# More of the attention's probability tiles transposed through memory, in a two-batch attention and LoRA block

## The chip, the core and the metric

One core of one Trainium2 chip runs the whole program in one launch. The metric is the device time of a run in microseconds (us). All data is float32.

## The reference

The input x is [2, 1024, 512]: two batches of 1024 tokens. The block is a pre-norm attention and a gated low-rank layer, both with a residual:

```
xn = layernorm(x)
q = rmsnorm(xn @ Wq.T), 32 heads of 128; k = rmsnorm(xn @ Wk.T), v = xn @ Wv.T, 8 heads of 128 (4 q heads share one)
scores = q @ k.T / sqrt(128) + slope[h] * (key - query), only keys <= query
x = x + (softmax(scores) @ v) @ Wo.T
f = layernorm(x); gates = 8 * softmax(f @ Wr.T + br)
x = x + 2 * sum_h gates[h] * (f @ A[h].T) @ B[h].T
```

## The kernel before

**Groups.** Each batch has 8 key/value heads, and each of them with its 4 query heads is one group of work: groups w = 0 to 7 are the first batch, 8 to 15 the second. In a group the 1024 queries are 8 row tiles s = 0 to 7 of 128. For row s and head h, `scores` (PE; every product is recorded at L1077, the line of the helper that issues it) fills PSUM with s + 1 blocks of 128 keys, `max` (DVE, L972) adds the bias and takes the row maximum, `exp` (ACT, L773) exponentiates and sums, `invert` (DVE, L979) takes the reciprocal for two heads at a time, and `normalise` (POOL, L852) multiplies. Every matrix product is three matmuls in a rounded float32 form (fp32r): each operand is split into a high part and a low rest, and high x high, high x low and low x high are summed.

**A probability tile.** The product with v needs the probabilities with keys on the partitions. So block j of row s, for the four heads together 128 x 512, has to be transposed. There are 36 such tiles in a group, and each goes one of two ways:

- on PE: `turn.p.s.j` (L1164) is four 128 x 128 transposes into a PSUM bank, `high.p` (ACT, L760) copies it rounded, `low.p` (DVE, L950) subtracts for the rest. It uses one of 2 slots of the pair of buffers pT_hi and pT_lo.
- through memory: `send_p.s.h` (SP's queue, L615) writes head h of all of the row's tiles of this kind to a buffer in device memory, one DMA for each head. `fetch_p.s.j` (SP's queue, L626) waits until all four heads of the row have landed and reads the tile back as 32 x 32 blocks put in transposed places, in 4 DMAs of 64 KB in runs of 128 bytes, to a raw buffer. `flip_p` (DVE, L958) transposes within the 32 x 32 blocks, `upper_p` (ACT, L768) and `lower_p` (POOL, L858) make the two parts. Here the first batch has 3 raw buffers and 2 slots, the second 5 and 4. A fetch waits for the `lower_p` that last read its raw buffer, an `upper_p` for the `values` item that last read its slot.

The table MEMORY_TILES says which tiles of a row go through memory: 16 of 36 in each group of the first batch, 20 of 36 in the second. `values.s.j` (PE) is three matmuls of 512 columns that add the tile's part to o_ps; in a row the tiles that PE transposed come first. Then `o_high` (ACT, L794) and `o_low` (DVE, L1000) split the result, and `y.s` (PE) is 12 matmuls of 512 columns against Wo, added up by `add_y` (L1006).

**Work of the next group.** A group also makes the next group's q (`q.8.c` and `q.9.c`: its first two rows, each in four items of 3 matmuls), and k and v (`turn.kv.0` to `3`, 24 matmuls of 256 columns each, then `turn.k.0`, `turn.k.1`). `v_high` and the next group's `values` wait for the last `values` of this one, since v has one buffer. The first batch transposes the weights on PE (10 items `turn.wo`, `turn.wkv`, `turn.wq`) and keeps them in memory; the second reads them back.

**The order.** Nothing is scheduled at run time: PROLOGUE, GROUP_A (groups 0 to 6), BOUNDARY (group 7), FIRST_B (8), GROUP_B (9 to 14) and LAST (15) are lists of items, and `follow` gives every engine those of its own kind in the list's order. Each engine runs its queue in order and waits where an item's inputs aren't there. BOUNDARY also has the second batch's layernorm and the first one's FFN, FIRST_B a rest of that FFN, and LAST the second one's. The FFN's tensors arT, bT and f_x are first used in BOUNDARY, where `load_a` and `load_wr` (SP's queue, L644 and L647) start.

**Head and tail.** This text calls the stretch of a group from its first matmul of `scores.0.0` to the end of `scores.7.3` its head, and from there to the next group's `scores.0.0` its tail.

Of the kernel before, what the change touches and what calls it, by code (L numbers as in the profile page):

```python
# [1261 lines left out]
```

## Time and profile before

| what | value |
|---|---|
| runs: median (lowest to highest of 3) | 2074.18 us (2071.1 to 2074.81) |
| the profiled execution: its own time | 2071.61 us |
| its span, first to last instruction | 2069.8 us |
| busy: PE, DVE, ACT, POOL | 97%, 66%, 56%, 56% |
| mean busy share of the 16 DMA engines, two queues | 37.8% (SP's) + 14.2% (ACT's) |
| the chain that ended last: PE | 79% |
| granted TensorE clock, mean | 0.997 |

PE's busy time counts matmuls whose ends are modelled: back to back, a matmul's duration overlaps the next one's, so work is better read from the spacing of starts. A wait of a few tenths can hide in it. In a timeline, consecutive instructions of one kind are merged (x4 is four), and idle time in front of them stands in brackets with what ended it.

### The profile page before, as it was taken

The numbers are of one execution on the slowest core, as the hardware profiler recorded it, in microseconds if no ns is written. First come the engines' busy times: TensorE is split into PE (matmuls) and PEld (weight loads), VectorE is DVE, ScalarE is ACT, GpSimd is POOL, SyncE is SP. The second block draws the span as 40 slices with busy tenths as digits, with TensorE's granted clock in tenths as the row PEclk, the third lists the DMA queues.
The fourth block names the chain that finished last, engine by engine and source line by source line (L and its number), as shares of the span: only waits on it lengthen the run. The fifth ranks groups of instructions, "written<-read, shape, count | busy, mean of one in ns | idle before, by whom it ended". The sixth has DMA issues, their size and how long they took to land.

```text
span 2069.8 us, 33617 instructions
## 1 busy us (share of the span) xinstructions
...
## 2 busy tenths in 40 slices
...
GB/s 163 120 135 110 166 122 131 106 125 171 107 144 138 97 158 115 146 151 153 122 131 140 136 99 175 99 151 142 108 138 99 176 102 142 154 77 167 70 124 93
DMA packets 822668, 269.13 MB, mean 130 GB/s; under 512 B 618584, under 2 KB 766040, under 8 KB 822496
## 3 DMA queue, kind: packets, MB, share of 16 engines
q1 hardware_dynamic: 770592, 164.75, 37.8%
q10 hardware_dynamic: 51904, 102.24, 14.2%
...
HBM read 145.25 MB, written 121.63 MB: 129 GB/s over the span
## 4 chain that ended last, share of the span: by engine, by line
PE 79%; DVE 6%; issue 4%; SPq 3%; DMA 3%; POOL 3%; ACT 2%; DVEq 0%; POOLq 0%; ACTq 0%
PE s_ps L1077 17%; PE q_ps L1077 15%; PE o_ps L1077 14%; PE y_ps L1077 14%; PE turn_ps L1164 10%; PE turn_ps L1077 7%; SPq L626 3%; DMA p_bounce<-probs_odd 1%; POOL probs_odd L852 1%; DVE more_raw L958 1%; DVE p_raw L958 1%; DVE qn L983 1%; DMA more_raw<-p_bounce 1%; POOL more_lo L858 1%; ACT qn L782 1%
## 5 line engine op out<-in xcount | busy, mean ns | idle before, releaser
L852 POOL TENSOR_TENSOR probs_odd<-probs_odd,p_inv 128x256 f32<-128x256 f32 (+3 forms) x256 | 316.6, 1255 | 212.4 <-DVE p_inv L979 212.4
L852 POOL TENSOR_TENSOR probs_even<-probs_even,p_inv 128x128 f32<-128x128 f32 (+3 forms) x256 | 261.6, 1043 | 222.0 <-DVE p_inv L979 221.7
L858 POOL TENSOR_TENSOR pT_lo<-p_raw,pT_hi 128x512 fp32r<-128x512 f32 x176 | 232.5, 1328 | 150.2 <-ACT pT_hi L768 150.0
L972 DVE CUSTOM_DVE_ANT_0 probs_odd<-s_ps,rel 128x256 f32<-128x256 f32 (+3 forms) x256 | 209.4, 820 | 107.4 <-issue 106.1
L1077 PE MATMUL s_ps<-kT_hi,qT_hi 128*128 128x512 f32 (+3 forms) x768 | 276.9, 361 | 2.9 <-DVE neg_max L972 2.8
L1077 PE MATMUL s_ps<-kT_hi,qT_lo 128*128 128x512 f32 (+3 forms) x768 | 262.3, 342 | 0.0
L1077 PE MATMUL s_ps<-kT_lo,qT_hi 128*128 128x512 f32 (+3 forms) x768 | 261.7, 341 | 0.0
L773 ACT ACTIVATE probs_odd<-probs_odd,neg_max 128x256 f32<-128x256 f32 (+3 forms) x256 | 212.4, 831 | 64.7 <-DVE neg_max L972 63.4
L773 ACT ACTIVATE probs_even<-probs_even,neg_max 128x128 f32<-128x128 f32 (+3 forms) x256 | 184.5, 722 | 108.7 <-DVE neg_max L972 106.9
L972 DVE CUSTOM_DVE_ANT_0 probs_even<-s_ps,rel 128x128 f32<-128x128 f32 (+3 forms) x256 | 174.8, 687 | 102.6 <-issue 101.7
L950 DVE TENSOR_TENSOR pT_lo<-turn_ps,pT_hi 128x512 fp32r<-128x512 f32 x288 | 195.2, 680 | 52.7 <-ACT pT_hi L760 52.5
L760 ACT ACTIVATE pT_hi<-turn_ps 128x512 fp32r<-128x512 f32 x288 | 169.7, 596 | 88.4 <-PE turn_ps L1164 88.3
L1077 PE MATMUL q_ps<-wqT_hi,xnT_hi 128*128 128x512 f32 x512 | 214.4, 419 | 0.1
L1077 PE MATMUL o_ps<-pT_hi,v_hi 128*128 128x512 f32 x496 | 205.9, 415 | 7.3 <-DVE oT_lo L1000 7.0
L1077 PE MATMUL y_ps<-woT_hi,oT_hi 128*128 128x512 f32 x512 | 204.5, 399 | 6.8 <-DVE oT_lo L1000 5.5
L1077 PE MATMUL q_ps<-wqT_hi,xnT_lo 128*128 128x512 f32 x512 | 201.0, 393 | 0.0
L1077 PE MATMUL y_ps<-woT_hi,oT_lo 128*128 128x512 f32 x512 | 200.8, 392 | 0.0
L1077 PE MATMUL y_ps<-woT_lo,oT_hi 128*128 128x512 f32 x512 | 200.8, 392 | 0.0
L1077 PE MATMUL q_ps<-wqT_lo,xnT_hi 128*128 128x512 f32 x512 | 200.5, 392 | 0.0
L782 ACT ACTIVATE qn<-q_ps 128x128 f32<-128x128 f32 x512 | 134.7, 279 | 107.2 <-PE q_ps L1077 105.7
L1077 PE MATMUL o_ps<-pT_hi,v_lo 128*128 128x512 f32 x496 | 194.6, 392 | 0.0
L1077 PE MATMUL o_ps<-pT_lo,v_hi 128*128 128x512 f32 x496 | 194.2, 391 | 0.0
...
## 6 DMA issues: line engine op xcount, KB each, us to landing
...
more_raw<-p_bounce SPq DMA_DIRECT2D x256, 64.0 KB, 2.2
...
```

The costliest lines, as they stand in the source:

```text
L626: sp.dma_start(raw_p(n)[b * BLOCK:(b + 1) * BLOCK, :].rearrange("p (n j) -> p n j", j=BLOCK), blocks[b]).then_inc(p_fetched[n], 16)
L760: nc.scalar.activation(target, bank, ACT.Copy).then_inc(sems["high"], 1)
L773: nc.scalar.activation(row, row, ACT.Exp, bias=neg_max[:, s % 2, h:h + 1], scale=-1.0, accum_out=p_sum[:, s % 2, h:h + 1]).then_inc(sems[" ...
L782: last = nc.scalar.activation(qn[:, h, :], q_ps[:, h * HD:(h + 1) * HD], ACT.Square, scale=float(slopes[gg % NG * G + h]), accum_out=q_sum ...
L852: nc.gpsimd.tensor_tensor(row, row, p_inv[:, s % 2, h:h + 1].to_broadcast((P, L)), ALU.mult).then_inc(sems["normalise"], 1)
L858: nc.gpsimd.tensor_tensor(p_low(r), raw_p(raw_tile[w, s, j]), p_high(r).bitcast(F32), ALU.subtract).then_inc(sems["lower_p"], 1)
L950: nc.vector.tensor_tensor(target, bank, upper.bitcast(F32), ALU.subtract).then_inc(sems["low"], 1)
L958: nc.vector.transpose(raw, raw).then_inc(sems["flip_p"], 1)
L972: nc.vector.tensor_tensor_reduce(out=probs[s % 2][:, h, 0:L], in0=s_ps[:, at_col:at_col + L], in1=rel[:, S - L:S], scale=-float(slopes[w % ...
L983: nc.vector.tensor_tensor(qn[:], q_ps[:].rearrange("p (h d) -> p h d", h=G), q_inv[:].unsqueeze(2).to_broadcast((P, G, HD)), ALU.mult).the ...
L1077: last = nc.tensor.matmul(target, a, m, start=start and i == 0 and k == 0, stop=stop and i == len(pairs) - 1 and k == 2)
L1164: last = nc.tensor.transpose(bank[0:width, i * rows:(i + 1) * rows], source, ident[0:rows, 0:rows])
```

## The change

Three things.

First, MEMORY_TILES has three stages in place of two: groups 0 to 6 now send 20 of 36 tiles through memory (16 before), group 7 keeps its 16, groups 8 to 15 send 24 (20 before). In groups 0 to 6, `turn.p` 4.2, 5.2, 6.3 and 7.2 go from PE to memory; in groups 8 to 15, 2.1, 3.1, 6.2 and 7.1.

Second, groups 0 to 6 get two more raw buffers and one more slot, in the room of f_x, bT and arT, which are not in use yet (5 raw buffers and 3 slots). `load_a` and `load_wr` therefore wait for the last readers of those places in group 6. Group 7 has 3 raw buffers and 2 slots as before, the second batch 5 and 4 as before.

Third, all six lists have a new order. Their other items are the same ones, each as often as before.

```diff
-MEMORY_TILES = ({2: (2,), 3: (2, 3), 4: (3, 4), 5: (3, 4, 5), 6: (4, 5, 6), 7: (3, 4, 5, 6, 7)},
-                {2: (2,), 3: (2, 3), 4: (2, 3, 4), 5: (2, 3, 4, 5), 6: (3, 4, 5, 6), 7: (2, 3, 4, 5, 6, 7)})
+MEMORY_TILES = ({2: (2,), 3: (2, 3), 4: (2, 3, 4), 5: (2, 3, 4, 5), 6: (3, 4, 5, 6), 7: (2, 3, 4, 5, 6, 7)},
+                {2: (2,), 3: (2, 3), 4: (3, 4), 5: (3, 4, 5), 6: (4, 5, 6), 7: (3, 4, 5, 6, 7)},
+                {2: (1, 2), 3: (1, 2, 3), 4: (2, 3, 4), 5: (2, 3, 4, 5), 6: (2, 3, 4, 5, 6), 7: (1, 2, 3, 4, 5, 6, 7)})
...
-    MEMORY_SLOTS, RAW_TILES = (2, 4), (3, 5)
+
+    MEMORY_SLOTS, RAW_TILES = 2, 3
+    MORE_SLOTS, MORE_RAW = (1, 0, 2), (2, 0, 2)
...
+    def stage(w):
+
+        return 0 if w < NG - 1 else 1 if w < NG else 2
...
+    def place(n, of, always, more):
+
+        n %= always + more[of]
+        return n if n < always else n + sum(more[:of])
...
+        with nc.sbuf_tensor("f_x", [P, 2, DM], F32) as f_x, nc.sbuf_tensor("bT", [P, DM], F32) as bT, \
+                nc.sbuf_tensor("arT", [P, C, P + NE], F32) as arT:
+            pass
+        pairs_0 = [(sb(f"pT_hi_a{i}", [P, G * P], F32R), sb(f"pT_lo_a{i}", [P, G * P], F32R)) for i in range(MORE_SLOTS[0])]
+        raw_0 = [sb(f"p_raw_a{i}", [P, G * P]) for i in range(MORE_RAW[0])]
...
+        def ffn_place_free(engine):
+            for name in last_early_slots:
+                after(engine, "values", *name)
+            for name in last_early_raws:
+                after(engine, "lower_p", *name)
...
             def load_a(w):
+                ffn_place_free(sp)
...
             def load_wr(w):
+                ffn_place_free(sp)
```

Of the lists, the end of GROUP_B, first before, then after:

```diff
-    "values.5.4 max.7.3 fetch_p.6.6 normalise.7.1 turn.p.6.0 turn.p.6.1 exp.7.3 y.4 send_p.7.0 send_p.7.1 high.p.6.0 "
-    "invert.7.1 flip_p.6.3 normalise.7.2 upper_p.6.3 values.5.5 add_y.4 normalise.7.3 turn.kv.3 send_p.7.2 low.p.6.0 "
-    "o_high.5 square_q.8 o_low.5 flip_p.6.4 high.p.6.1 lower_p.6.3 send_p.7.3 low.p.6.1 values.6.0 flip_p.6.5 "
-    "high.kv.3 inv_q.8 turn.p.6.2 low.kv.3 values.6.1 high.p.6.2 inv_k fetch_p.7.2 y.5 upper_p.6.4 low.p.6.2 "
-    "upper_p.6.5 norm_q.8 flip_p.6.6 lower_p.6.4 fetch_p.7.3 norm_k upper_p.6.6 values.6.2 lower_p.6.5 turn.p.7.0 "
-    "fetch_p.7.4 values.6.3 flip_p.7.2 lower_p.6.6 values.6.4 upper_p.7.2 q.9.0 high.p.7.0 fetch_p.7.5 lower_p.7.2 "
-    "values.6.5 flip_p.7.3 low.p.7.0 values.6.6 q.9.1 fetch_p.7.6 o_high.6 turn.p.7.1 upper_p.7.3 o_low.6 q.9.2 "
-    "high.p.7.1 lower_p.7.3 add_y.5 values.7.0 fetch_p.7.7 low.p.7.1 y.6 flip_p.7.4 flip_p.7.5 upper_p.7.4 "
-    "upper_p.7.5 lower_p.7.4 flip_p.7.6 values.7.1 lower_p.7.5 add_y.6 values.7.2 flip_p.7.7 turn.q.8 upper_p.7.6 "
-    "values.7.3 lower_p.7.6 values.7.4 upper_p.7.7 values.7.5 high.q.8 lower_p.7.7 values.7.6 low.q.8 turn.k.0 "
-    "values.7.7 high.k.0 turn.k.1 o_high.7 q.9.3 v_high o_low.7 high.k.1 y.7 v_low square_q.9 low.k.0 inv_q.9 low.k.1 "
-    "add_y.7 "
...
+    "send_p.7.0 exp.7.3 send_p.7.1 values.5.4 fetch_p.6.5 invert.7.1 flip_p.6.2 normalise.7.2 values.5.5 low.kv.2 "
+    "q.8.2 o_high.5 q.8.3 high.p.6.0 normalise.7.3 send_p.7.2 upper_p.6.2 low.p.6.0 turn.kv.3 high.p.6.1 flip_p.6.3 "
+    "add_y.4 upper_p.6.3 lower_p.6.2 send_p.7.3 o_low.5 fetch_p.6.6 flip_p.6.4 lower_p.6.3 values.6.0 low.p.6.1 "
+    "upper_p.6.4 turn.p.7.0 flip_p.6.5 square_q.8 lower_p.6.4 fetch_p.7.1 y.5 high.kv.3 inv_q.8 upper_p.6.5 "
+    "fetch_p.7.2 high.p.7.0 lower_p.6.5 norm_q.8 values.6.1 low.kv.3 values.6.2 inv_k fetch_p.7.3 low.p.7.0 "
+    "values.6.3 flip_p.6.6 turn.q.8 flip_p.7.1 upper_p.6.6 values.6.4 fetch_p.7.4 norm_k upper_p.7.1 lower_p.6.6 "
+    "q.9.0 high.q.8 values.6.5 lower_p.7.1 values.6.6 flip_p.7.2 fetch_p.7.5 turn.k.0 flip_p.7.3 upper_p.7.2 turn.k.1 "
+    "o_high.6 q.9.1 lower_p.7.2 high.k.0 o_low.6 fetch_p.7.6 q.9.2 upper_p.7.3 flip_p.7.4 values.7.0 lower_p.7.3 "
+    "upper_p.7.4 q.9.3 high.k.1 fetch_p.7.7 values.7.1 lower_p.7.4 flip_p.7.5 values.7.2 low.q.8 upper_p.7.5 "
+    "values.7.3 add_y.5 lower_p.7.5 values.7.4 flip_p.7.6 y.6 upper_p.7.6 lower_p.7.6 flip_p.7.7 low.k.0 upper_p.7.7 "
+    "low.k.1 lower_p.7.7 values.7.5 add_y.6 values.7.6 values.7.7 o_high.7 square_q.9 o_low.7 v_high y.7 inv_q.9 "
+    "v_low add_y.7 "
```

## Rows read from the trace of the kernel before

**Rows 1.** Windows: group 1, the turn of the batches, groups 8 and 15; columns as headed
```profile
core 0: us, PE busy (x) PEld busy (x) DVE busy (x) ACT busy (x) POOL busy (x), PEclk, DMA share, GB/s
...
166.60:291.80 125.20, 124.42 (x702) 107.30 (x701) 82.06 (x199) 74.09 (x210) 67.80 (x66) 1.00 0.51 131
...
917.20:1063.50 146.30, 142.23 (x812) 120.37 (x811) 123.53 (x319) 77.16 (x224) 78.62 (x94) 1.00 0.52 138
1063.50:1190.20 126.70, 124.13 (x676) 104.92 (x675) 83.97 (x216) 69.39 (x203) 75.50 (x75) 1.00 0.58 144
...
1924.20:2069.80 145.60, 125.48 (x633) 99.31 (x632) 107.83 (x291) 65.20 (x179) 74.91 (x81) 0.96 0.44 102
```

**Rows 2.** Windows: head of group 14; tails of groups 10, 11, 12, 14, 4 and 8
```profile
1801.90:1888.60 86.70, 85.83 (x478) 74.87 (x478) 55.12 (x156) 51.54 (x155) 49.97 (x52) 1.00 0.52 132
...
1398.88:1435.12 36.24, 34.09 (x169) 27.77 (x167) 21.41 (x32) 17.05 (x44) 23.53 (x20) 0.95 0.62 126
1521.88:1556.12 34.24, 32.81 (x168) 26.47 (x167) 21.29 (x32) 17.17 (x44) 23.52 (x20) 1.00 0.62 129
1642.88:1679.61 36.73, 32.98 (x168) 26.48 (x167) 21.29 (x32) 16.95 (x44) 23.50 (x20) 1.00 0.59 122
...
1888.64:1924.23 35.59, 32.69 (x168) 26.58 (x167) 21.29 (x32) 16.95 (x44) 23.54 (x20) 1.00 0.56 109
630.22:667.57 37.35, 36.81 (x220) 32.04 (x219) 23.20 (x35) 18.41 (x47) 19.61 (x17) 1.00 0.46 104
1157.32:1190.17 32.85, 31.50 (x150) 24.82 (x149) 21.74 (x32) 17.26 (x42) 22.68 (x19) 1.00 0.64 131
```

**Rows 3.** Groups of instructions: shapes xcount | busy, mean ns | idle before it, releaser
```profile
L858 POOL TENSOR_TENSOR pT_lo<-p_raw,pT_hi 128x512 fp32r<-128x512 f32 x176 | 232.5, 1328 | 150.2 <-ACT pT_hi L768 150.0
...
L950 DVE TENSOR_TENSOR pT_lo<-turn_ps,pT_hi 128x512 fp32r<-128x512 f32 x288 | 195.2, 680 | 52.7 <-ACT pT_hi L760 52.5
...
L760 ACT ACTIVATE pT_hi<-turn_ps 128x512 fp32r<-128x512 f32 x288 | 169.7, 596 | 88.4 <-PE turn_ps L1164 88.3
L958 DVE STREAM_TRANSPOSE p_raw<-p_raw 128x512 f32<-128x512 f32 x224 | 155.5, 699 | 39.6 <-DMA p_raw<-p_bounce 39.6
...
L768 ACT ACTIVATE pT_hi<-p_raw 128x512 fp32r<-128x512 f32 x176 | 110.6, 630 | 131.0 <-DVE p_raw L958 78.4 <-PE o_ps L1077 52.1
...
L1164 PE MATMUL turn_ps<-ident,probs_odd 128*128 128x128 f32 x608 | 90.4, 274 | 7.8 <-DVE probs_odd L888 7.8
```

**Rows 4.** Timeline of PE, group 9: start us, us, operation xcount
```profile
1302.12 0.60 PE L1164 MATMUL turn_ps<-ident,qn 128*128 128x128 f32 x4
1302.48 0.48 PE L1077 MATMUL o_ps<-more_hi,v_hi 128*128 128x512 f32 x1
1302.79 0.40 PE L1077 MATMUL o_ps<-more_lo,v_hi 128*128 128x512 f32 x1
1303.03 0.39 PE L1077 MATMUL o_ps<-more_hi,v_lo 128*128 128x512 f32 x1
```

**Rows 5.** Timeline of SP's queue, group 14: sends and fetches of the last row
```profile
1893.13 3.35 SPq L615 DMA_DIRECT2D p_bounce<-probs_odd  x4
...
1900.54 2.75 SPq L626 DMA_DIRECT2D more_raw<-p_bounce  x4
...
1909.77 4.15 SPq L626 DMA_DIRECT2D more_raw<-p_bounce  x8
```

**Rows 6.** Timeline of SP's queue: the same fetches in groups 10, 11, 8 and 4
```profile
1412.15 1.91 SPq L626 DMA_DIRECT2D more_raw<-p_bounce  x4
...
1533.40 1.91 SPq L626 DMA_DIRECT2D more_raw<-p_bounce  x4
...
1164.54 4.64 SPq L626 DMA_DIRECT2D more_raw<-p_bounce  x8
...
639.53 14.84 SPq L626 DMA_DIRECT2D p_raw<-p_bounce  x20
```

**Rows 7.** Timeline of PE, group 14: the last values item
```profile
1919.00 0.50 PE L1077 MATMUL o_ps<-more_hi,v_hi 128*128 128x512 f32 x1 [1.23 <-POOL more_lo L858]
```

More of the change, by code:

```diff
@@ L335, in attention_lora_block @@
         plans.setdefault(w, group_a if w < NG else group_b)
+    def stage(w):
+        return 0 if w < NG - 1 else 1 if w < NG else 2
     def through_memory(w, s):
-        return list(MEMORY_TILES[w // NG].get(s, ()))
+        return list(MEMORY_TILES[stage(w)].get(s, ()))
     def values_order(w, s):
@@ L386, in attention_lora_block @@
     turned, sends = [], [0, 0]
-    flips, fetches, last_in_slot, in_raw = [0, 0], [0, 0], {}, {}
+    flips, fetches, last_in_slot, in_raw = [0] * 3, [0] * 3, {}, {}
+    def place(n, of, always, more):
+        n %= always + more[of]
+        return n if n < always else n + sum(more[:of])
     for w in range(-1, LAST_W + 1):
@@ L393, in attention_lora_block @@
             elif item[0] == "flip_p":
-                name, b = (w, *item[1:]), w // NG
-                p_slot[name] = TURN_SLOTS + flips[b] % MEMORY_SLOTS[b]
+                name, of = (w, *item[1:]), stage(w)
+                p_slot[name] = TURN_SLOTS + place(flips[of], of, MEMORY_SLOTS, MORE_SLOTS)
                 p_before[name] = last_in_slot.get(p_slot[name])
                 last_in_slot[p_slot[name]] = name
-                flips[b] += 1
+                flips[of] += 1
             elif item[0] == "send_p" and item[2] == G - 1:
@@ L402, in attention_lora_block @@
             elif item[0] == "fetch_p":
-                name, b = (w, *item[1:]), w // NG
-                raw_tile[name] = fetches[b] % RAW_TILES[b]
+                name, of = (w, *item[1:]), stage(w)
+                raw_tile[name] = place(fetches[of], of, RAW_TILES, MORE_RAW)
                 users = in_raw.setdefault(raw_tile[name], [])
@@ L408, in attention_lora_block @@
                 raw_uses[name] = len(users)
-                fetches[b] += 1
+                fetches[of] += 1
     def follow(work):
@@ L498, in attention_lora_block @@
             pass
-        more_hi = sb("more_hi", [P, 2, G * P], F32R)
-        more_lo = sb("more_lo", [P, 2, G * P], F32R)
-        more_raw = sb("more_raw", [P, 2, G * P])
+        pairs_2 = [(sb(f"pT_hi_b{i}", [P, G * P], F32R), sb(f"pT_lo_b{i}", [P, G * P], F32R)) for i in range(MORE_SLOTS[2])]
+        raw_2 = [sb(f"p_raw_b{i}", [P, G * P]) for i in range(MORE_RAW[2])]
+        with nc.sbuf_tensor("f_x", [P, 2, DM], F32) as f_x, nc.sbuf_tensor("bT", [P, DM], F32) as bT, \
[3 more added lines that the diff above has]
+        raw_0 = [sb(f"p_raw_a{i}", [P, G * P]) for i in range(MORE_RAW[0])]
+        sb("arT_rest", [P, C * (P + NE) - W512])
+        turned_pairs = [(pT_hi[:, i, :], pT_lo[:, i, :]) for i in range(TURN_SLOTS + MEMORY_SLOTS)]
+        turned_pairs += [(hi[:], lo[:]) for hi, lo in pairs_0 + pairs_2]
+        raws = [p_raw[:, i, :] for i in range(RAW_TILES)] + [raw[:] for raw in raw_0 + raw_2]
         b_raw = f_x[:, 0, :].rearrange("p (h o r) -> p h o r", o=C, r=RK)
@@ L508, in p_high @@
         def p_high(slot):
-            more = slot - TURN_SLOTS - MEMORY_SLOTS[0]
-            return pT_hi[:, slot, :] if more < 0 else more_hi[:, more, :]
+            return turned_pairs[slot][0]
         def p_low(slot):
-            more = slot - TURN_SLOTS - MEMORY_SLOTS[0]
-            return pT_lo[:, slot, :] if more < 0 else more_lo[:, more, :]
+            return turned_pairs[slot][1]
         def raw_p(n):
-            return p_raw[:, n, :] if n < RAW_TILES[0] else more_raw[:, n - RAW_TILES[0], :]
+            return raws[n]
+        early = [name for name in p_slot if name[0] < NG - 1]
+        last_early_slots = [[name for name in early if p_slot[name] == TURN_SLOTS + MEMORY_SLOTS + i][-1] for i in range(MORE_SLOTS[0])]
+        last_early_raws = [[name for name in raw_tile if name[0] < NG - 1 and raw_tile[name] == RAW_TILES + i][-1] for i in range(MORE_RAW[0])]
+        def ffn_place_free(engine):
[3 more added lines that the diff above has]
+                after(engine, "lower_p", *name)
         def x_source(b, t):
@@ L550, in attention_lora_block @@
         p_sent = [sem("p_sent_even"), sem("p_sent_odd")]
-        p_fetched = [sem(f"p_fetched{i}") for i in range(RAW_TILES[1])]
+        p_fetched = [sem(f"p_fetched{i}") for i in range(RAW_TILES + sum(MORE_RAW))]
         ident_ready = sem("ident_ready")
```

10 lines of the change are left out of this document (3 added, 7 removed), and 502 rows, old and new, of tables (BOUNDARY, FIRST_B, GROUP_A, GROUP_B).

## The prediction, made before the changed kernel ran

> **What bounds the kernel now.** I read the windows first, by group. PE is busy for 124.4 of the 125.2 us of a first-batch group, for 124.1 of 126.7 in group 8, and for 125.5 of 145.6 in group 15, whose end is a serial chain of the FFN [rows 1]. So PE sets the pace, and an instruction taken off PE pays, as long as PE doesn't then wait for what replaces it. I then cut the groups in two. A second-batch head takes 86.7 us and PE is idle for 0.9 of it; a second-batch tail takes 34.2 to 36.7 us, mean 35.7 of four shown, with 1.4 to 3.7 idle; a first-batch tail takes 37.35 with 0.5 idle [rows 2]. The heads repeat, the tails scatter: what varies is there. The timelines say why. The last `values` item of group 14 starts at 1919.00 after a wait for `lower_p` [rows 7], 30.36 us after `scores.7.3` ended at 1888.64 [rows 2]. Behind it lies row 7's way through memory: four sends, then nothing from SP until they have landed, then 24 fetches one after the other [rows 5]. The first batch is bound by PE's work, the second by PE's work plus a late last row.
>
> **What four tiles less cost PE.** The timeline shows one turn between matmuls [rows 4]: four transposes at 1302.12, the next matmul at 1302.48, the one after it 0.31 later where 0.24 is usual. That is 0.36 + 0.07 = 0.43 to 0.44 us for a tile. 28 tiles in the first batch and 32 in the second make 60 x 0.44 = 26.4 us, 1.76 a group: the gain if nothing new waits. The mean duration of one transpose is 274 ns [rows 3], but durations overlap, so I don't take it. The Trainium skill (TensorE: Matmul & The Clock Gate, Part 4: PE-mode transpose) gives about 275 ns for a transpose in one kernel's context; as the price of each of the 240 transposes that would be a gain of 66 us. The duration agrees, but the spacing of the starts is what PE gets back.
>
> **What replaces them.** On ACT 630 ns for 596, on DVE 699 ns for 680 [rows 3]: nothing, neither is the pace. On POOL 1.33 us a tile, new [rows 3]: 5.3 us a group on top of 67.8 in 125.2 [rows 1], covered by its idle time; should a `lower_p` stand before a `normalise` that PE awaits, it costs up to 1.33 there. On SP's queue a fetch is four issues: eight take 4.15 us [rows 5], with the gap 2.1 us a tile, or 8.5 us a group, and row 7's and others' sends grow by a sixth or so. SP only matters where a row waits for it, which is row 7. `load_a` and `load_wr` now wait, with group 7's loads and first sends queued behind them, for the last `values` of group 6 at most; group 7's first tile through memory belongs to row 2, many us later, so I take nothing for these two waits.
>
> **Row 7's chain.** From `scores.7.3` to the first fetch (call it F) group 14 takes 1900.54 - 1888.64 = 11.9 us; group 10 13.3, group 11 11.5 [rows 2, 5, 6]. What follows `values.7.7` in a tail is 35.59 - 30.36 = 5.2 us. So F to `values.7.7` is 18.5, 17.7 and 17.5 us, 17.9 on average with six tiles; a seventh adds 2.1. Two groups start earlier: group 4 at 639.53 - 630.22 = 9.3 us, and group 8, whose second four of eight issues at 1164.54 begin about 1167, at 9.7 [rows 2, 6]. In the list of group 8 `fetch_p.6.6` stands behind `send_p.7.3`, so it goes out while the sends travel; in GROUP_B it stood ahead of `send_p.7.0`. The new GROUP_B has it behind `send_p.7.3`, and `fetch_p.6.5` behind `send_p.7.1`. But row 6 has five fetches now, as many before the last send as before. The new F lies between group 8's 9.7 and the old mean of 12.2; I take 10.8, nearer to the order that it has.
>
> **Groups 9 to 14.** I count PE's items from `scores.7.3` to `values.7.7` in both lists. Before: 16 `values` (0.69 each, three starts of 0.23), 3 `y` (2.74), one `turn.kv` (2.8), 3 `q` (0.69), 7 turns (0.44) make 27.2 us, and the trace's 30.36 is that plus the waits. After: 6 `q` and 4 turns make 28.0. Two `q` items and two turns changed sides, so the head gets shorter by 1.4 and by nothing else. The chain needs 10.8 + 17.9 + 2.1 = 30.8 us against 30.4 in group 14 (and 35.7 - 5.2 = 30.5 in the mean of the four). That is over the 28.0 of work, so PE still waits there: the chain sets it, not the work. A group changes by -1.4 + 0.4 = -1.0 us, six by -6. The bounds: F at 9.7 gives -2.1 a group, which its present waits allow; F at 12.2 gives +0.4, at 13.3 +1.5. In the new order `y.7` follows `values.7.7` with nothing between; before, a turn and a `q` lay there. From the one to the other it was 5.2 - 2.7 = 2.5 us, of which the matmuls, `o_high` and `o_low` take 0.7 + 0.6 + 0.7 in a row (the last two like the same operations in [rows 3]), so `y.7` waited for `o_low` then too, and the empty place costs nothing more.
>
> **Groups 0 to 6.** The tail now has 29.5 us of PE work to `values.7.7`, counted the same way. Its chain is F = 9.3 to 9.7, plus 17.9 with six tiles and five raw buffers, as the second batch has: 27.6 us. It is covered by work, and the whole 1.76 comes out. Against that `load_wo` (1 MB) moves down next to row 6's fetches and `keep_wkv` up into the tail. The old trace doesn't show this meeting; the nearest rows are the spread of F in the second batch, up to 13.3. F over 11.6 would begin to cost. I take off 0.16: -1.6 a group, -11.2 for seven. Bounds -12.4 and, with F at 13.3 (31.2 us, the old tail's own), about 0.
>
> **The rest.** Group 8: by count the head is 5 us shorter and the tail has 7 tiles at F = 9.7, so 29.7 for 27.6 us; as at most 1.8 of work and its 2.6 idle can go [rows 1], I take -2 (0 to -3). Group 15: head 2.3 shorter, of which 1.8 is work; its seventh tile gives 1 back: -1.3 (+1 to -2.3). Group 7 has the same work in a new order and is idle for 4.1 us [rows 1]: 0, between -2 and +2. The prologue's new order of loads: 0, within 1.
>
> **The sum.** -11.2 - 6 - 2 - 1.3 = -20.5 us against the profiled execution's own 2071.6 (span 2069.8), so 2051. The runs' median lies 2.6 above that execution; for the median I say 2074.2 - 20.5 = **2053.7 us**, a ratio of 0.990.
>
> **Rivals.**
> - *The full price.* F falls to 9.7 in every second-batch group and nothing meets `load_wo`: -12.4, six times -1.8 to -2.1, -3, -2.3: about -29, 2045 us. For it: F in groups 4 and 8, and that the heads repeat. Against it: a longer send (seven tiles) and five fetches in row 6. 0.20.
> - *Given back in the tails.* F stays at 12.2 in the second batch: +0.4 x 6, groups 8 and 15 even, and the first batch gets half (-6): about -4 to -2, 2071 us. For it: the old tails, where all that scatters depends on this queue. 0.16.
> - *SP's queue becomes the bound (slower).* The fetches and sends of row 6 push F past 13; at 14 a regular group pays 14 + 20 - 30.4 - 1.4 = +2.2 us, six make 13, groups 8 and 15 another 4, and the first batch gives 11 of that back: +6, 2080 us; with the first batch's tail held up too, 2085. It decides at F of about 13, where eight groups lose what seven gain; group 10 was there [rows 6]. 0.12. The Trainium skill (VectorE: DVE Perf Modes, Rules for kernel authors) says to transpose 128 x 128 on TensorE where the result may go to PSUM, which speaks against this change. No row here shows a tile slower as such, only its last steps late.
> - That the change doesn't do what it says is unlikely: by count each GROUP list loses four turns and gains four of each item through memory.
>
> My forecast has 0.52.
>
> **The numbers.** A measurement of this kernel can tell about 0.2%, 4 us, from no change. Faster by more than that takes the forecast, the full price and a little of the third case: 0.76. Within it most of the third: 0.13. Slower: 0.11. The range runs from the full price with a small bonus in group 7, 2043, to the third case, 2071; my case's own range is 2048 to 2062.
>
> **What would show it.** Right: periods of 123.5 us in groups 0 to 6 with F near 9.5 and no wait before `values.7.7`; heads of 85.3 us in groups 9 to 14, F of 10 to 11.5, `values.7.7` at 30 to 31.5 us after `scores.7.3` and still waiting for `lower_p`; PE's starts 240 fewer; POOL busy 80 us more. Wrong: F at 12 or more, waits in the heads (a `values.2.1` or `values.3.1` that comes before its tile), POOL's `normalise` behind a `lower_p`, or a first-batch tail that waits for a fetch.

## The result: 1.2% slower, and the profile after

The changed kernel takes 2097.7 us (median of 4 runs, 2095.9 to 2099.1) against 2072.6 us (4 runs, 2069.4 to 2074.8) on the same chip: a ratio of 1.0122, 95% interval 1.0104 to 1.014. The forecast was 2053.7 us in a range up to 2071. The profiled execution has a span of 2094.7 us and a time of 2096.5, 24.9 more than the one before.

First the page of the changed kernel: instructions, SP's queue (q1), and the chain that ended last by engine and by line.

```profile
PE 2003.9 (96%) x10828; PEld 1696.4 (81%) x10828; DVE 1365.4 (65%) x3431; ACT 1161.2 (55%) x3314; POOL 1237.7 (59%) x1220
...
q1 hardware_dynamic: 928032, 196.22, 44.8%
...
PE 53%; SPq 15%; DMA 9%; issue 7%; DVE 7%; POOL 5%; ACT 3%; DVEq 0%; POOLq 0%; ACTq 0%
SPq L656 14%; PE s_ps L1109 13%; PE q_ps L1109 11%; PE y_ps L1109 10%; PE o_ps L1109 8%; PE turn_ps L1196 7%; DMA p_bounce<-probs_odd 4%; PE turn_ps L1109 3%; DMA p_bounce<-probs_even 2%; POOL probs_odd L884 2%; POOL probs_even L884 1%; DMA p_raw<-p_bounce 1%; SPq L645 1%; DMA p_raw_a<-p_bounce 1%; POOL pT_lo L890 1%
```

PE has its 240 starts fewer (11068 before) and POOL its 60 more, as the diff says. What is new is in the chain: PE's share was 79% and is 53%; SP's queue and the DMAs had 3% each and have 15% and 9%. `SPq L656` is the issuing of fetches. A quarter of the chain now runs through SP's queue and the DMAs instead of through PE's work.

Then the windows, by group: groups 1 and 2, 7, 8, 9, 12 and 15 of the changed kernel. The columns are those of [rows 1].

```profile
164.40:289.20 124.80, 123.31 (x686) 105.75 (x684) 81.82 (x199) 73.78 (x210) 73.61 (x70) 1.00 0.60 148
289.20:417.60 128.40, 123.76 (x688) 105.86 (x686) 81.84 (x199) 73.81 (x210) 73.59 (x70) 1.00 0.59 144
918.10:1062.00 143.90, 141.57 (x812) 120.14 (x811) 120.58 (x319) 77.66 (x224) 79.20 (x94) 1.00 0.50 130
1062.00:1193.70 131.70, 125.54 (x660) 105.29 (x659) 83.23 (x216) 69.25 (x203) 80.00 (x78) 0.97 0.67 166
1193.70:1319.50 125.80, 119.30 (x629) 100.63 (x628) 75.90 (x188) 69.21 (x199) 78.24 (x74) 0.99 0.62 145
1571.40:1696.70 125.30, 120.07 (x629) 101.75 (x628) 75.79 (x188) 69.16 (x199) 78.19 (x74) 0.97 0.62 143
1947.30:2094.70 147.40, 126.80 (x617) 98.64 (x616) 107.33 (x291) 65.18 (x179) 80.27 (x84) 0.95 0.50 115
```

Summed from the first `scores` of each group to that of the next, in both profiled executions: the prologue gains 1.5 us and group 7 gains 2.4; groups 0 to 6 take 878.1 us against 875.6 (+2.5); group 8 131.7 against 126.7 (+5.0); groups 9 to 14 753.7 against 734.1 (+19.6, 3.3 each); group 15 147.4 against 145.6 (+1.8). Together +25. (Groups 0 to 6 with this same list took 869.1 to 878.1 us in the twelve profiles that have it here, 873.6 on average; with the old list 875.6 and 876.1. So the first batch usually gives 2 us back, and this execution is its worst.) PE is idle for 5 to 6.5 us in a second-batch group.

The head of group 12, its tail, and the tails of groups 14 and 2:

```profile
1571.36:1657.22 85.86, 84.75 (x472) 73.53 (x471) 54.55 (x155) 52.03 (x155) 52.54 (x53) 1.00 0.57 140
1657.22:1691.45 34.23, 31.53 (x143) 25.41 (x141) 19.32 (x31) 14.54 (x34) 24.44 (x20) 0.90 0.75 142
...
1908.97:1942.09 33.12, 29.30 (x144) 23.05 (x142) 19.35 (x31) 14.55 (x34) 24.43 (x20) 1.00 0.76 145
377.30:411.52 34.22, 30.28 (x173) 25.80 (x171) 18.37 (x30) 14.95 (x48) 22.27 (x18) 1.00 0.74 154
```

These tails run from the end of `scores.7.3` to the start of `values.7.7`. Group 14's is 33.12 us where it was 30.36, and only 0.8 us of that is more work by the prediction's count (28.0 against 27.2). The heads are near the forecast (85.4 to 86.0 us in groups 9 to 14; 85.3 was said). So in these groups the loss is in the tails.

SP's queue says why. Group 12 of the changed kernel, where `scores.7.3` ended at 1657.22:

```profile
1655.06 4.05 SPq L656 DMA_DIRECT2D p_raw_b<-p_bounce  x8
1659.21 2.02 SPq L656 DMA_DIRECT2D p_raw<-p_bounce  x4
1661.34 1.04 SPq L645 DMA_DIRECT2D p_bounce<-probs_odd  x2
1662.48 3.56 SPq L656 DMA_DIRECT2D p_raw<-p_bounce  x4
1666.08 1.13 SPq L645 DMA_DIRECT2D p_bounce<-probs_odd  x2
1667.30 4.00 SPq L656 DMA_DIRECT2D p_raw<-p_bounce  x4
1672.04 4.02 SPq L656 DMA_DIRECT2D p_raw_b<-p_bounce  x8
```

Four issues are one fetch. Between 1655.06 and 1661.23 stand three fetches of row 6; the first two sends of row 7, whose first tile was normalised 0.3 us after `scores.7.3`, leave only at 1661.34, 4.1 after it. Then one more fetch of row 6, the last two sends at 1666.08, one more fetch, and at 1672.04 the first of row 7. F, from `scores.7.3` to there, is 14.8 us. A fetch that stands behind sends also takes longer to issue: 3.56 and 4.00 us for four, against 2.02. Over the six groups F is 13.4 to 14.8, 14.2 on average, where the kernel before had 11.5 to 13.3, 12.3 on average; in group 8 it is 16.7.

What ends F is told by the landings. The trace has the last send landed 0.01 to 0.02 us before the first fetch of row 7 in each of the six groups, and SP was through with issuing only 0.1 to 0.8 us before that: two things end almost together. The issue of the last send ends 10.1 us after `scores.7.3` on average (8.4 in the kernel before), and it lands 4.0 us later (3.8 before). The raw buffers are not what holds it. The first tile of row 7 takes the raw buffer of 6.2 now, but the `lower_p` that it waits for had ended 8.0 us after `scores.7.3` in all six groups.

The clock makes it a little worse. `y.7` of group 13, behind its wait for `o_low` (PE's timeline, and the window to the end of the group):

```profile
1819.13 0.50 PE L1109 MATMUL y_ps<-woT_hi,oT_hi 128*128 128x512 f32 x1 [1.41 <-DVE oT_lo L1032]
...
1820.32 0.63 PE L1109 MATMUL y_ps<-woT_lo,oT_hi 128*128 128x512 f32 x1
1820.74 0.63 PE L1109 MATMUL y_ps<-woT_hi,oT_lo 128*128 128x512 f32 x1
1821.17 0.63 PE L1109 MATMUL y_ps<-woT_hi,oT_hi 128*128 128x512 f32 x1
```
```profile
1819.10:1823.60 4.50, 4.47 (x13) 3.53 (x14) 1.23 (x1) 1.23 (x4) 1.21 (x2) 0.62 0.61 229
```

The starts are 0.43 us apart where 0.23 is usual: the granted clock fell to 1.2 GHz after a tail in which PE had waited, and these twelve matmuls cost 1.6 us more than in the groups without it. It happened in groups 11 and 13. Over the whole span the mean granted clock is 0.988, against 0.997. Where the fall lies inside a tail that waits anyway, as in group 12 (0.90), it costs little and fills the idle time: that tail shows only 2.7 us idle, group 14's at full clock 3.8.

### The profile page after: what moved, and what is told of

Read it like the earlier page. It is cut to its first block, busy times and chain, and to the rows that moved or that the text cites. A ratio compares the mean times of both kernels' runs of the same rounds, so it can differ in the third digit from the quotient of the medians.

```text
span 2094.7 us, 33555 instructions
## 1 busy us (share of the span) xinstructions
PE 2003.9 (96%) x10828; PEld 1696.4 (81%) x10828; DVE 1365.4 (65%) x3431; ACT 1161.2 (55%) x3314; POOL 1237.7 (59%) x1220
## 4 chain that ended last, share of the span: by engine, by line
PE 53%; SPq 15%; DMA 9%; issue 7%; DVE 7%; POOL 5%; ACT 3%; DVEq 0%; POOLq 0%; ACTq 0%
SPq L656 14%; PE s_ps L1109 13%; PE q_ps L1109 11%; PE y_ps L1109 10%; PE o_ps L1109 8%; PE turn_ps L1196 7%; DMA p_bounce<-probs_odd 4%; PE turn_ps L1109 3%; DMA p_bounce<-probs_even 2%; POOL probs_odd L884 2%; POOL probs_even L884 1%; DMA p_raw<-p_bounce 1%; SPq L645 1%; DMA p_raw_a<-p_bounce 1%; POOL pT_lo L890 1%
## 5 line engine op out<-in xcount | busy, mean ns | idle before, releaser
L1109 PE MATMUL s_ps<-kT_hi,qT_hi 128*128 128x512 f32 (+3 forms) x768 | 272.5, 355 | 3.2 <-DVE neg_max L1004 2.2
L890 POOL TENSOR_TENSOR pT_lo<-p_raw,pT_hi 128x512 fp32r<-128x512 f32 x129 | 167.8, 1306 | 110.8 <-ACT pT_hi L800 110.8
L1109 PE MATMUL y_ps<-woT_hi,oT_hi 128*128 128x512 f32 x512 | 205.8, 402 | 17.6 <-DVE oT_lo L1032 14.0
L1109 PE MATMUL q_ps<-wqT_hi,xnT_hi 128*128 128x512 f32 x512 | 218.6, 427 | 2.1 <-DVE qn L1015 2.1
L1109 PE MATMUL o_ps<-pT_hi,v_hi 128*128 128x512 f32 x434 | 183.2, 422 | 24.2 <-POOL pT_lo L890 15.0
L990 DVE STREAM_TRANSPOSE p_raw<-p_raw 128x512 f32<-128x512 f32 x216 | 150.7, 702 | 74.9 <-DMA p_raw<-p_bounce 74.0
L982 DVE TENSOR_TENSOR pT_lo<-turn_ps,pT_hi 128x512 fp32r<-128x512 f32 x228 | 155.5, 683 | 54.4 <-ACT pT_hi L792 53.9
L792 ACT ACTIVATE pT_hi<-turn_ps 128x512 fp32r<-128x512 f32 x228 | 134.6, 595 | 99.2 <-PE turn_ps L1196 98.9
L1109 PE MATMUL o_ps<-pT_hi,v_lo 128*128 128x512 f32 x434 | 172.3, 397 | 0.0
L1109 PE MATMUL o_ps<-pT_lo,v_hi 128*128 128x512 f32 x434 | 171.4, 395 | 0.0
```

The lines of the kernel that those rows point to most:

```text
L792: nc.scalar.activation(target, bank, ACT.Copy).then_inc(sems["high"], 1)
L890: nc.gpsimd.tensor_tensor(p_low(r), raw_p(raw_tile[w, s, j]), p_high(r).bitcast(F32), ALU.subtract).then_inc(sems["lower_p"], 1)
L982: nc.vector.tensor_tensor(target, bank, upper.bitcast(F32), ALU.subtract).then_inc(sems["low"], 1)
L990: nc.vector.transpose(raw, raw).then_inc(sems["flip_p"], 1)
L1109: last = nc.tensor.matmul(target, a, m, start=start and i == 0 and k == 0, stop=stop and i == len(pairs) - 1 and k == 2)
```

## The experiments

Ratios are to runs of the kernel before on the same chip. The change ran on another chip than the variants: the kernel before takes 2072.6 us there and 2069.7 to 2070.4 on theirs. Where a variant is compared with the change's 2097.7 us below, the gain is therefore 2 to 3.5 us smaller by the ratios. Three theories stood against each other: the queue theory (SP's queue issues the last row's sends and fetches late), the load theory (the core's DMA engines have too much to move in the tail, whichever queue it comes from), and the clock as a cause of its own.

### One batch alone, and two halves of the second batch

**e1_first_batch_only**: the lists and tables of groups 8 to 15 as before. **e2_second_batch_only**: the prologue and groups 0 to 7 as before. For e1:

```diff
-                {2: (1, 2), 3: (1, 2, 3), 4: (2, 3, 4), 5: (2, 3, 4, 5), 6: (2, 3, 4, 5, 6), 7: (1, 2, 3, 4, 5, 6, 7)})
+                {2: (2,), 3: (2, 3), 4: (2, 3, 4), 5: (2, 3, 4, 5), 6: (3, 4, 5, 6), 7: (2, 3, 4, 5, 6, 7)})
```

> Only the first batch has the change: PROLOGUE, GROUP_A, BOUNDARY and their table are the changed kernel's, FIRST_B, GROUP_B, LAST and the 20 tiles of groups 8 to 15 the old one's. Theory Q (the loss lies in the second batch's tails, where SP's queue issues the last row's sends and fetches too late): the parts of the first half, read from the two traces, are -1.5 us in the prologue, +2.4 in groups 0 to 6 and -2.4 in group 7, so 2071 us against 2072.6, a ratio of 0.998 to 1.001; the tails of groups 9 to 14 go back to 30.4 us from scores.7.3 to the last values item. Theory C (the loss is the lower TensorE clock, which comes with the smaller PE work anywhere): dips of the clock remain, half of the loss stays, about 2085 us.

> Only the second batch has the change (groups 8 to 15 with 24 tiles and their new lists; prologue, groups 0 to 7 as before). Theory Q: the whole loss, 5.0 us in group 8, 19.6 in groups 9 to 14 and 1.8 in group 15, so 2072.6 + 26 = 2099 us, a ratio of 1.012 to 1.014. Theory C, if the dips come from what the first batch does: half or less, 2085.

Measured: e1 2064.6 us, ratio 0.9973 (0.9958 to 0.9988); e2 2101.0 us, 1.0142 (1.012 to 1.0164). e1 is a little faster than its expectation (0.998 to 1.001), which took the first batch from the change's own execution, its worst. The clock theory's 2085 us is out for both: the first batch's part helps, the second's does all the harm. In e1 the first-batch groups come in two kinds: 123.65 us with F at 9.85 us, where no tail waits, and 125.3 to 127.2 with F at 11 to 13.9.

**e3_rows_2_3_back** and **e4_rows_6_7_back**: in groups 9 to 14 two of the four more tiles go back to PE, once the early ones (2.1 and 3.1), once the late ones (6.2 and 7.1). The tables of those groups:

```diff
 e3
-{2: (1, 2), 3: (1, 2, 3), 4: (2, 3, 4), 5: (2, 3, 4, 5), 6: (2, 3, 4, 5, 6), 7: (1, 2, 3, 4, 5, 6, 7)}
+{2: (2,), 3: (2, 3), 4: (2, 3, 4), 5: (2, 3, 4, 5), 6: (2, 3, 4, 5, 6), 7: (1, 2, 3, 4, 5, 6, 7)}
 e4
-{2: (1, 2), 3: (1, 2, 3), 4: (2, 3, 4), 5: (2, 3, 4, 5), 6: (2, 3, 4, 5, 6), 7: (1, 2, 3, 4, 5, 6, 7)}
+{2: (1, 2), 3: (1, 2, 3), 4: (2, 3, 4), 5: (2, 3, 4, 5), 6: (3, 4, 5, 6), 7: (2, 3, 4, 5, 6, 7)}
```

> The changed kernel, but in groups 9 to 14 tiles 2.1 and 3.1 are transposed on PE again; rows 6 and 7 keep their added tiles (22 through memory). Theory Q (only what SP issues around rows 6 and 7 counts): tails as in the changed kernel, 34.1 us from scores.7.3 to the last values item, and two turns more in each head, +0.9 us a group: 2097.7 + 5 = 2103 us. Theory L (the DMA engines' total load makes every transfer late): tails half-way back, 32.3 us, so 2092 us.

> The changed kernel, but in groups 9 to 14 tiles 6.2 and 7.1 are transposed on PE again; rows 2 and 3 keep their added tiles (22 through memory). Theory Q: first fetch of row 7 at 12 us after scores.7.3 and six tiles, so 30 to 31 us to the last values item, a group takes 121.5 to 122.5 us: 2097.7 - 6 x 3.6 = 2076 us. Theory L: half-way back, 2087 us. Were the lost time in the heads (rows 2 and 3 late), nothing would be won here: 2097 us or more.

Measured: e3 2104.3 us, 1.016 (1.0134 to 1.0186); e4 2067.9 us, 0.999 (0.9981 to 1.0). With two tiles fewer through memory in either, one mends nothing and the other gives back 30 us (27 by the ratios), 8 more than was expected. So it is not how much goes through memory in a group, but when. SP's queue in group 12 of e4 (`scores.7.3` ended at 1639.76):

```profile
1635.71 1.92 SPq L656 DMA_DIRECT2D p_raw<-p_bounce  x4
1637.72 2.02 SPq L656 DMA_DIRECT2D p_raw_b<-p_bounce  x4
1640.11 2.18 SPq L645 DMA_DIRECT2D p_bounce<-probs_odd  x2
1642.39 2.49 SPq L656 DMA_DIRECT2D p_raw_b<-p_bounce  x4
1644.93 1.97 SPq L645 DMA_DIRECT2D p_bounce<-probs_odd  x2
1647.00 7.71 SPq L656 DMA_DIRECT2D p_raw<-p_bounce  x12
```

The queue is through with two fetches of row 6 at 1639.74, before `send_p.7.0` is due, and each send leaves as its tile is normalised (0.35, 2.16, 5.17 and 6.76 us after `scores.7.3`). Row 7's first fetch is the second four of the last line, at 1650.2: F is 10.4. `values.7.7` then starts at 30.8 us without a wait of its own (PE is idle for 1.3 us of the tail, at two earlier `values` items), and groups 10 to 14 take 121.2 to 121.5 us at full clock; only group 9 takes 122.0. Over the six groups F is 9.9 to 11.0, 10.4 on average: the last send's issue ends 7.2 us after `scores.7.3`, and it lands 3.0 us later. e3's F is 13.6 to 14.8.

### The order of the queue

**e5_fetch_behind_sends** and **e6_sends_early** keep 24 tiles and change SP's order in groups 9 to 14 alone. SP's items from row 6's sends on:

```diff
 e5
 send_p.7.1
-fetch_p.6.5
 send_p.7.2
 send_p.7.3
+fetch_p.6.5
 fetch_p.6.6
 e6 (on top of e5)
 fetch_p.5.3
+send_p.6.0
 fetch_p.5.4
+send_p.6.1
 fetch_p.5.5
-send_p.6.0
-send_p.6.1
 send_p.6.2
 send_p.6.3
 fetch_p.6.2
 fetch_p.6.3
-fetch_p.6.4
 send_p.7.0
 send_p.7.1
+fetch_p.6.4
 send_p.7.2
```

> All of the change stays, 24 tiles too; only fetch_p.6.5 moves in the list of groups 9 to 14 from behind send_p.7.1 to behind send_p.7.3. Queue theory (what fetches stand ahead of row 7's last send sets F): send_p.7.3 goes out at 6.8 to 7.5 us after scores.7.3 instead of 9.5, F falls from 14.1 to about 11.5, values.7.7 comes at 31.5: 2.6 us a group less, 16 in all, about 2082, or 2077 if the half-speed stretches of the clock go with the waits. Load theory (the bytes and packets of 24 tiles keep the DMA engines busy, whatever the order): F stays within 0.5 of 14, 2095 to 2098.

> As the one before, with two more places changed: fetch_p.6.4 behind send_p.7.1, and send_p.6.0 and 6.1 ahead of fetch_p.5.4 and 5.5. Queue theory: all eight sends go out as their tiles are normalised, send_p.7.3 at 6.8; ahead of row 7 still stand two or three fetches of row 6 (2.1 us each), so F is 11 to 12.5 and the time 2076 to 2082; the sends were not the larger part, the fetches are. Load theory: 2095 to 2098.

Measured: e5 2095.4 us, 1.0122 (1.0103 to 1.0141); e6 2093.9 us, 1.0112 (1.0091 to 1.0133). Both expectations of the queue theory missed. Group 12 of e5 (`scores.7.3` ended at 1652.81):

```profile
1656.66 3.67 SPq L645 DMA_DIRECT2D p_bounce<-probs_odd  x4
1660.43 7.63 SPq L656 DMA_DIRECT2D p_raw<-p_bounce  x8
1668.16 4.15 SPq L656 DMA_DIRECT2D p_raw_b<-p_bounce  x8
```

The last send left at 1659.57, 6.76 us after `scores.7.3` and as early as it can; but the two fetches behind it took 7.63 us to issue where eight issues take 4.15 in the next line, and F is 15.4. The sends had landed 1.3 us before that, so here it is the queue alone that ends F. In e6 the two fetches took 6.01 us and F is 13.4:

```profile
1663.17 6.01 SPq L655 DMA_DIRECT2D p_raw<-p_bounce  x8
```

What stood before the sends now stands behind them, stretched. Over the six groups F is 14.7 on average in e5 and 13.1 in e6, of 14.2. So the order is worth at most 1.1 us of F, while taking one fetch out (e12, below) is worth 3.3. e6 won its 1.1 us in the tails and lost them elsewhere: its heads are 1.3 us longer (PE is idle for 1.6 to 3.0 us of each, 0.9 to 1.2 in the change), and `y.7` ran at half clock in four groups instead of two.

### The same bytes on two queues

Both are e4 with 256 KB more in each of groups 9 to 14, in runs of 128 bytes, from a weight in memory to a scratch in memory that nobody reads: on SP's queue as four DMAs, or on ACT's as one.

```diff
 e7, in send_p
+                if (s, h) == (NT - 1, 2) and NG < w < LAST_W:
+                    for b in range(NBLK):
+                        sp.dma_start(extra[b * BLOCK:(b + 1) * BLOCK, :].rearrange("p (n j) -> p n j", j=BLOCK),
+                                     Wq[0:W512, b * BLOCK:(b + 1) * BLOCK].rearrange("(n b) j -> b n j", b=BLOCK)).then_inc(extra_done, 16)
 e8, in exp
+                if (s, h) == (NT - 1, 3) and NG < w < LAST_W:
+                    act.dma_start(extra.rearrange("p (n j) -> p n j", j=BLOCK),
+                                  Wq[0:16 * P, 0:BLOCK].rearrange("(n b) j -> b n j", b=P)).then_inc(extra_done, 16)
```

> The variant with 22 tiles in groups 9 to 14 (2067.9 us) plus, ahead of send_p.7.2 in each of these six groups, four extra DMAs on SP's queue of 64 KB in runs of 128 bytes (DRAM to DRAM, data that nobody uses): the issue work and the bytes of one fetch. Queue theory: send_p.7.2 and 7.3 and all behind them are 2.1 us later, 12.6 us in all, 2080. Load theory: the same, since the bytes are the same.

> The same 256 KB in runs of 128 bytes at the same moment, but issued as one DMA by ACT ahead of exp.7.3 instead of four on SP. Queue theory: SP's queue holds nothing more, so F stays at 10 to 11 and the time at 2067 to 2071; only what ACT itself loses to issuing counts. Load theory: as the one before, about 2080, since the DMA engines have the same packets to move at the same moment.

Measured: e7 2080.3 us, 1.0043 (1.0026 to 1.006); e8 2069.0 us, 0.9993 (0.9983 to 1.0002). On SP's queue the four cost 12.4 us, on ACT's the one cost 1.1, which is inside the spread of e4's runs. Queue and number of DMAs changed together; four DMAs of 64 KB on ACT's queue were not tried here. Group 12 of e7 (`scores.7.3` ended at 1647.93):

```profile
1653.10 3.42 SPq L650 DMA_DIRECT2D extra<-in_L_attn_Wq  x4
1656.57 1.21 SPq L653 DMA_DIRECT2D p_bounce<-probs_odd  x2
1657.87 7.57 SPq L664 DMA_DIRECT2D p_raw<-p_bounce  x12
```

F is 12.8 to 14.1 in e7 and 10.2 to 11.5 in e8. The total of e7 is what was expected, but not by that sum: since 2 us of F were covered in e4, `values.7.7` is only 0.0 to 2.0 us later, 4.6 in all six groups. Another 5.5 came in `y.7` of groups 11, 13 and 14, which ran at half clock (1.6 us in each of the first two), and 2.6 in group 8, where nothing had been added.

### Two fetches on ACT's queue, and one tile at a time

**e9_two_fetches_on_act** keeps 24 tiles and issues `fetch_p.6.5` and `6.6` from ACT in groups 9 to 14.

```diff
 e9, in the functions of SP and of ACT
+    ON_ACT = ((6, 5), (6, 6))
             def fetch_p(w, s, j):
+                if (s, j) in ON_ACT and NG < w < LAST_W:
+                    return
+            def fetch_p(w, s, j):
+                if (s, j) in ON_ACT and NG < w < LAST_W:
+                    fetch_on(act, w, s, j)
```

> The change as it is, 24 tiles, but in groups 9 to 14 the eight DMAs of fetch_p.6.5 and 6.6 are issued by ACT, behind exp.7.3, instead of SP. If it is SP's own queue that is full (what its order could not mend), F falls by the two fetches, from 14.1 to 10 to 11, values.7.7 comes at 30.5 to 31.5 instead of 33.5, and the time is 2075 to 2082; ACT has 4.2 us of issuing more, which it has free time for. If what counts is the packets that the core's DMA engines must move in those microseconds, whichever queue they come from, F stays near 14 and the time at 2094 to 2098.

Measured: 2083.0 us, 1.0067 (1.005 to 1.0085), 14.8 less than the change as it is (11 by the ratios). That is 1 us outside what the queue theory gave for the time (2075 to 2082), and F, 12.8 to 14.0, is well outside what it gave for that (10 to 11). The load theory's time (2094 to 2098) is missed by 11. Group 12 (`scores.7.3` ended at 1651.48), SP's queue and ACT's:

```profile
1655.68 4.14 SPq L657 DMA_DIRECT2D p_bounce<-probs_odd  x4
1664.48 4.04 SPq L624 DMA_DIRECT2D p_raw_b<-p_bounce  x8
```
```profile
1653.01 1.41 ACTq L624 DMA_DIRECT2D p_raw<-p_bounce  x3
1654.45 2.83 ACTq L624 DMA_DIRECT2D p_raw<-p_bounce  x5
```

The sends are all issued by 1659.82 and then SP has nothing to issue for 4.7 us: it waits for the sends to land. F is 13.0, of 14.8; over the six groups 13.3, of 14.2. The last send is issued 1.9 us earlier than in the change (8.3 us after `scores.7.3`, not 10.1), but it takes 5.0 us to land instead of 4.0. So the issuing could be taken from SP's queue, and half of what that gave was lost in the landing. `values.7.7` comes 1.2 us earlier, 7 us in six groups. The rest of the gain can't be read from this profile, which is of the slowest of e9's four runs. The windows of the 14 us behind `scores.7.3` in group 12 show the DMA engines, in the changed kernel and in e4:

```profile
1657.22:1671.22 14.00, 14.00 (x76) 12.02 (x75) 7.94 (x15) 7.10 (x22) 11.10 (x10) 1.00 0.92 204
```
```profile
1639.76:1653.76 14.00, 13.75 (x76) 11.71 (x75) 8.16 (x15) 7.10 (x22) 11.77 (x11) 1.00 0.84 181
```

The engines are busy for 0.92 of it instead of 0.84. But that share alone doesn't make F late. The same 14 us of e8, in two halves, have more of it (0.95 on average) with F at 10.7:

```profile
1637.56:1644.56 7.00, 7.00 (x39) 6.07 (x38) 3.58 (x8) 3.08 (x6) 5.88 (x4) 1.00 1.03 213
1644.56:1651.56 7.00, 6.74 (x40) 5.63 (x39) 4.57 (x8) 4.03 (x17) 5.89 (x7) 1.00 0.88 189
```

The Trainium skill (DMA: Bandwidth & Descriptors, Issuing engines are not separate DMA queues) says that DMAs from any engine run on the same 16 DMA engines, and that spreading them saves only the sequencer's issue time. e7 and e8 agree: the same bytes held SP's queue for 3.42 us and cost 12.4 us in all, and from ACT they cost nothing clear of the noise. So does e9: the sends left earlier and did not land faster. Why they landed 1.0 us slower there stays open.

**e12_row_6_back** and **e13_row_7_back**: the two late tiles of e4, one at a time.

```diff
 e12
-6: (2, 3, 4, 5, 6), 7: (1, 2, 3, 4, 5, 6, 7)}
+6: (3, 4, 5, 6), 7: (1, 2, 3, 4, 5, 6, 7)}
 e13
-6: (2, 3, 4, 5, 6), 7: (1, 2, 3, 4, 5, 6, 7)}
+6: (2, 3, 4, 5, 6), 7: (2, 3, 4, 5, 6, 7)}
```

> In groups 9 to 14 only tile 6.2 goes back to PE (row 6 fetches four, row 7 still seven). If the fifth fetch of row 6 delays the first of row 7 (F 14 to 11 or 12) and the seventh of row 7 adds 2.1 us behind it, values.7.7 comes at 31 to 32 us, each group is 2 to 3 us shorter and its half-speed stretches mostly go: 2078 to 2084. If row 7's seventh tile is the whole trouble, F stays at 14 and the time at 2093 to 2098.

> In groups 9 to 14 only tile 7.1 goes back to PE (row 6 still fetches five, row 7 six). F stays at 13.5 to 14 by either reading; values.7.7 comes one fetch (2.1 us) earlier, at 31.3 to 32: 2080 to 2086. If the fifth fetch of row 6 alone were the trouble, nothing would be gained: 2093 to 2098. Together with the run before: if the two tiles' costs add up, the two gains sum to the 30 us that both gave; if either alone brings the chain back under PE's work, the two gains sum to more.

Measured: e12 2075.8 us, 1.0026 (1.0012 to 1.0039); e13 2080.1 us, 1.005 (1.0033 to 1.0067). 21.9 and 17.6 us less than the change: together 39.5, more than the 29.8 of both (by the ratios 35 against 27, which is just outside the noise). e12 is 2 us better than expected, e13 inside. In e12, whose group 12 is shown (`scores.7.3` ended at 1637.50), F is 10.6 to 11.3 although row 7 still sends and fetches seven, and `values.7.7` starts at 30.0 to 31.3; in e13 F stays at 13.1 to 14.5 and `values.7.7` comes at 30.7 to 32.2. So it is row 6's fifth tile that makes F, and giving back either tile alone brings the chain nearly under PE's work.

```profile
1643.04 1.59 SPq L645 DMA_DIRECT2D p_bounce<-probs_odd  x2
1644.74 6.25 SPq L656 DMA_DIRECT2D p_raw_b<-p_bounce  x8
```

The second four of the last line are row 7's first fetch. Groups 9 to 14 took 735.7 us in e12's profile and 728.7 in e4's; about 6 of these 7 us are the half clock in `y.7` of groups 9, 11, 12 and 13. (e12's profile is of its fastest run, 2068.1 us; what the slower ones add isn't shown.)

### What the first batch was missing, and a version that beats both

**e10_load_wo_early** is e1 with one item moved in the list of groups 0 to 6; **e11_22_tiles_old_ends** is the first batch as changed, e4's groups 9 to 14, and groups 8 and 15 with their old lists and 20 tiles; **e14_22_tiles_load_wo** is both.

```diff
 e10 and e14, GROUP_A
 fetch_p.5.3
+load_wo
 fetch_p.5.4
...
 send_p.6.3
-load_wo
 fetch_p.6.3
```

> The first batch new and the second old (2064.6 us as it was), with load_wo back near its old place in the list of groups 0 to 6, behind fetch_p.5.3. Theory: load_wo's 1 MB meets row 6's sends and fetches and makes about every second group late; with it early, F is 9.9 in all seven groups and each takes 123.7 us instead of a mean of 125.0: about 9 us less, 2056. If the lateness comes from the four more tiles themselves and load_wo has no part, the time stays at 2062 to 2067 with the same two kinds of groups.

> The first batch as changed; groups 9 to 14 with 22 tiles (rows 2 and 3 as changed, rows 6 and 7 as before); groups 8 and 15 with their old lists and 20 tiles. From the parts measured so far: first batch alone 2064.6, and groups 9 to 14 with 22 tiles took about 4 us less than with 20: 2061, 0.9955 of the kernel before. If the parts do not add up (the clock's half-speed stretches move about), 2063 to 2067.

> The kernel with 22 tiles in groups 9 to 14, 20 elsewhere and the old lists of groups 8 and 15 (2061.2 us), with load_wo early in groups 0 to 6. If the two parts add up: 2.5 us less, 2058.7, 0.994 to 0.995 of the kernel before. If load_wo's place only spread the lateness evenly: 2061.

Measured: e10 2062.0 us, 0.9968 (0.9958 to 0.9978); e11 2061.2 us, 0.9958 (0.9947 to 0.997); e14 2058.6 us (6 runs, 2054.4 to 2061.5), 0.9946 (0.9932 to 0.996). Moving `load_wo` took the two kinds of first-batch groups away but did not bring all to 123.65: F is 10.7 to 11.9 in each, groups take 123.9 to 125.1. The 9 us that the theory gave for it are 2.6, and the two intervals overlap: e10's own step is not shown to be more than nothing. Nor is it in e14, whose interval overlaps e11's: groups 0 to 6 take 869.0 us in e14's profile, and 869.5 and 869.1 in those of e11 and e12, where `load_wo` has not moved. In e14's profile group 7 takes 143.9 us, group 8 127.0 and groups 9 to 14 728.1; with groups 0 to 6 that is 6.6, 2.4, -0.2 and 5.9 less than before, and no group from 9 to 14 ends at half clock. It is 39 us faster than the change (36 by the ratios), and 12 faster than the kernel before, which is what e14 shows: 22 tiles in groups 9 to 14 and 20 in groups 0 to 6 and in 8 and 15 are better than either kernel.

## Why the prediction was wrong

- **What four tiles less cost PE.** Right in kind, a little large. Where the tail doesn't wait (e1, F 9.85) a first-batch group takes 123.65 us against 125.2: 1.55 for four tiles, 0.39 each, where 0.44 was read from [rows 4]. The heads of groups 9 to 14 came at 85.4 to 86.0, said 85.3: 1.0 less than before, said 1.4. The price read from the spacing of starts held; 275 ns for each transpose, 1.1 us a tile, would have been nearly three times the truth.
- **What replaces them.** POOL is busy for 78.8 us more (80 said), and neither it nor ACT nor DVE became the pace. Nothing to mend there.
- **Row 7's chain: the step that failed.** "But row 6 has five fetches now, as many before the last send as before. The new F lies between group 8's 9.7 and the old mean of 12.2; I take 10.8, nearer to the order that it has." It came at 13.4 to 14.8, 14.2 on average. For row 6 with four fetches the reading of the order was right: e4, in the new order, has 10.4. The fifth tile is what I took at almost nothing, and it costs 3.3 to 3.7 (e12: F back to 10.6 to 11.3). The fetch that stands behind the last send is indeed nearly free, since SP is through with it 0.1 to 0.8 us before the sends have landed. But four still stand ahead of that send, as in the kernel before, and with as many ahead it can't leave earlier than it did. Its issue ends at 10.1 us, against 8.4 before and 7.2 in e4. Row 6's sends carry five tiles and land later, so that its fetches begin 2.4 us before `scores.7.3` on average, not 3.4 as in e4 or 3.7 as before; and the fetch between the sends takes 3.6 to 4.2 us to issue, where I had 2.1. Then the last send needs 4.0 us to land (3.0 in e4). e5 and e6, two other orders, don't mend it: F counts all that the queue passes before row 7's first fetch. Behind F the chain was right: 19.9 us to `values.7.7` on average of the six groups, 20.0 said.
- **Groups 9 to 14.** Said -1.0 each, measured +3.3. `values.7.7` came 34.1 us after `scores.7.3` on average of the six instead of 30.4 (+3.7), the heads are 1.0 shorter (1.4 said), and the half clock in `y.7`, which no step had, adds 3.2 us in two groups, 0.5 a group: +3.2 of the 3.3.
- **Groups 0 to 6.** Said -1.6 each; +0.35 in this execution, -0.3 on average of the twelve profiles with this list. The slack was put at F = 11.6, and e1's late groups cross that (F up to 13.9). That `load_wo` would meet row 6 there was named, but at a price of 0.16; what the meeting costs isn't shown, since e10 moved `load_wo` and won 2.6 us at most of the 9. The failing step is the same one: row 6 went from three fetches to four here, and F from 9.3 to 9.6 in the old list to anything between 9.8 and 14.8 in the profiles with the new one.
- **Groups 8, 15, 7 and the prologue.** Group 8: said -2 with F = 9.7, measured +5.0 with F = 16.7: the same failed step, in its new list; with its old list and 20 tiles it takes 127 us (e11, e14). Group 15: said -1.3, +1.8. Group 7 and the prologue gave 2.4 and 1.5 us, each about half a microsecond outside its bound (2 and 1).
- **The rivals.** The slower one, SP's queue as the bound, had 0.12 and is what happened, with its place (F over 13) right and its price too low, 2080 to 2085 for 2097.7: it let the first batch keep its gain (or half of it), priced groups 8 and 15 at 4 us together where they cost 6.8, and had no clock in it. "Given back in the tails" and it together deserved most of the chance: the old groups 10 and 14 with F of 13.3 and 11.9 [rows 5, 6] were the warning that this queue had no room.
